# Second angle table from an absolute value on ScalarE, FiLM read from PSUM, and new turns in a two-layer decoder kernel

## The chip, the cores and the metric

The kernel runs on one core of a Trainium2 chip. Its engines are named as the profile names them: PE (TensorE, matrix products), DVE (VectorE), ACT (ScalarE), POOL (GpSimd) and SP (SyncE, which issues DMAs). The metric is the device time of one execution in microseconds; the kernel before took 485.99 us (median of 3 runs, 484.13 to 487.59). Lower is better.

## The reference, cut to what matters

Two sequences of 512 tokens with 128 features go through two post-norm decoder layers. Layer 0: a Hawk recurrent block, cross attention to a short context, and latent attention with a mixture of 7 routed experts and a shared one. Layer 1: a selective scan with 16 states, a state-space cross layer, and a mixture of 8 routed experts and shared ones. After each part stands `x = _layernorm(x + part(x))`. The change lies in the state-space layer:

```
c_t = jnp.einsum('btg,bgd->btd', attn_mean, V)
x = layernorm(x_text, g_norm_in, b_norm_in)
scale_in, shift_in = jnp.split(c_t @ W_film_in + b_film_in, 2, axis=-1)
x = x * (1.0 + mod_gate * scale_in) + mod_gate * shift_in
powers = jnp.exp(dtA[:, :, None] * jnp.arange(L))      # s4d: 64 complex poles per feature
K = 2.0 * jnp.einsum('dn,dnl->dl', dC, powers).real    # 512 taps per feature
y = irfft(rfft(x, n=2 * L) * rfft(K, n=2 * L)) + x * D_skip
scale_out, shift_out = jnp.split(c_t @ W_film_out + b_film_out, 2, axis=-1)
y = y * (1.0 + mod_gate * scale_out) + mod_gate * shift_out
xt = x_text + y
```

The 512 taps K depend on weights alone. [...]

## The kernel before, in words

The two sequences are two **lanes**, a (or 0) and b (or 1); what depends on weights alone is a third, w. A lane's activations stand as 128 features by 512 tokens, in float32, in sixteen tiles of 128 x 512 (`A(b, i)`, in the trace AR; the layer's input is x_in or `Xin`), and each lane owns four banks of PSUM (`own(b, i)`, in the trace PS). RR is a large shared tile that holds the taps' tables and, later, weights.

Each engine's work is a list of named **steps** for each lane (`STEPS`, `STEPS_W`). `TURNS` says for each engine which lane gives its next steps ("a8 w1" is eight steps of lane a, then one of w), and so fixes the engine's order for the whole program; an engine that waits in one lane holds up the others behind it. Every step counts up a semaphore of its engine and lane, and `after(engine, lane, step)` is the wait for it. `TABLES` says ahead of which ACT step a set of activation functions is loaded (42 loads, before as after). Nothing is scheduled at run time.

```
for n, lane in enumerate(lanes_):
    before(n)
    next(programs[lane])
```

Helpers record most instructions on one line each: on ACT L1208 (table loads L1204), on DVE L1553 (two tensors), L1556 (tensor and scalar), L1559 (`stt`, scalar and two tensors), L1562 (reductions), L1565 (reciprocal), L1878 (the selective scan), on POOL L2195 and L2279 (one tensor in pieces of 128 x 512).

**The taps' tables** (lane w, two halves h = 0, 1, each 128 x 1024 and larger). POOL forms angles, `tP` and `tQ`. DVE rounds them to whole turns: `r1`, `q1` (phase 1 into tile p1), `r2`, `q2` (phase 2 into p2), then `rQ0`, `qQ0`, `rQ1`, `qQ1`; an `r` is L1556, a `q` L1559. ACT takes sines (`s1`, `s2`, `sQ`) and exponentials (`eP`, `eQ`). POOL forms `aP`, `aQ`, `U1`, `U2`, `V`, `Q`; DVE `P`. PE sums them to taps (`kp`); taps go through a DMA (`kshuf`, into `Kdl`), PE transposes them (`kt`, L1184) and takes their spectrum (`kf`, L1008).

**The selective scan** of layer 1, per lane and state: ACT an exponential, DMA spreads a row, POOL a product `by` (L2195, after one product `dx`), DVE the scan `sc` (L1878) and a product `hc` (L1553). Lane 1's experts of layer 0 (DVE `hu`, `hw`; PE `fg`, `fu`, `fd`) run beside lane 0's scan, lane 0's state-space layer beside lane 1's scan.

**The state-space layer**, per lane: context attention (`xb.s` ... `xb.p`, whose result is transposed, `xb.t`, L1032); four products with the FiLM weights (`fl0` to `fl3`, L1039), which ACT copies from PSUM with their bias (`s0` to `s3`); DVE `lni.z` and `xin` apply scale and shift to the normed input; PE transposes (`xit`, L1045) and takes the spectrum (`xf`, L1008); DVE multiplies it with the taps' (`xr`, `xi`, `yr`, `yi`, `ye`, `yo`); PE goes back (`inv0`, `inv`, L1061, even and odd tokens in one bank); DVE adds the skip (`sk`, L1559), scales (`fo`), shifts (`fp`) and adds the residual (`xta`, `xt`). The feed-forward part and two layer norms follow (`lnf`, `w1`, `w2`, `lno`, `ln5`; L1067, L1075, L1083, L689), then the second mixture (L1096 its router, L925, L930 and L957 its experts).

## Time and profile before

| What | Value |
|---|---|
| runs | 487.59, 485.99, 484.13 us; median 485.99 |
| profiled execution | 481.76 us; span 480.0 us, 5922 instructions |
| PE busy | 411.1 us (86%) x2035 |
| DVE busy | 331.9 us (69%) x616 |
| ACT busy | 289.2 us (60%) x508, of it 42 table loads 53.9 us |
| POOL busy | 124.9 us (26%) x128 |
| chain that ended last | PE 59%; DVE 21%; ACT 10%; issue 6% |
| mean granted clock of TensorE | 0.932 |

The span runs from the first to the last instruction of the profiled execution; the runs were timed apart from it. A busy share near the length of a stretch says that the engine sets the pace there; the granted clock is a share of TensorE's full speed, so that 0.82 over a stretch means that part of it ran at the lower of its two levels. A row of a timeline may join several like instructions (x2), and its bracket tells how long the engine had been idle and what ended that.

### The profile page before, as it was taken

To read this page: it belongs to the slowest core of one execution; us is meant where nothing else is said; L and a number is where in the kernel's file an instruction comes from. 1 tells how busy PE (TensorE), PEld (TensorE's weight loads), DVE (VectorE), ACT (ScalarE), POOL (GpSimd) and SP (SyncE) were. 2 spreads that over 40 slices of the span, in tenths; PEclk is the share of its full clock that TensorE was granted. 3 is DMA by queue.
4 is the path that set the end of the run, shared out by engine and by line. 5 is a ranking of instruction groups with operands and counts; after the bars stand their busy time and mean duration, and the time that the engine had idled before them with its cause. 6 is when DMAs were issued, how large, how long until landed. Compare 5 with 4: busy or idle time off the path is not lost.

```text
span 480.0 us, 5922 instructions
## 1 busy us (share of the span) xinstructions
PE 411.1 (86%) x2035; PEld 201.5 (42%) x2035; DVE 331.9 (69%) x616; ACT 289.2 (60%) x508; POOL 124.9 (26%) x128
## 2 busy tenths in 40 slices
PE   6978988878799999999977884557889899999995
PEld 3444433443345554434443221233666544544442
DVE  1485567799969963562799999899977543574454
ACT  5945697525255678989567897456347576552125
POOL 1200000000482029006965767745100200000000
PEclk9988999988879999999997998657989999999999
DMA  7950000564281000005008967988600001502401
GB/s 262 362 157 32 1 2 0 164 98 152 70 182 17 2 3 4 2 12 165 0 1 231 233 164 222 217 223 253 252 0 1 1 0 22 156 1 54 124 0 44
DMA packets 26109, 46.62 MB, mean 97 GB/s; under 512 B 7397, under 2 KB 12742, under 8 KB 24918
## 3 DMA queue, kind: packets, MB, share of 16 engines
q1 hardware_dynamic: 25972, 46.15, 33.7%
q8 instruction: 16, 0.26, 0.2%
q10 hardware_dynamic: 108, 0.10, 0.1%
q14 instruction: 13, 0.11, 0.1%
HBM read 41.13 MB, written 5.01 MB: 96 GB/s over the span
## 4 chain that ended last, share of the span: by engine, by line
PE 59%; DVE 21%; ACT 10%; issue 6%; POOL 2%; DMA 1%; DVEq 0%; SPq 0%; ACTq 0%
PE PS L925 7%; DVE AR L1553 7%; PE PS L957 6%; ACT AR L1208 6%; PE PS L930 5%; PE PS L853 4%; PE PS L839 4%; ACT L1204 3%; PE PS L689 3%; PE PS L822 3%; DVE stats L1562 3%; DVE AR L1878 3%; PE PS L1008 2%; PE PS L1061 2%; DVE AR L1559 2%
## 5 line engine op out<-in xcount | busy, mean ns | idle before, releaser
L1208 ACT ACTIVATE AR<-PS 128x512 f32<-128x512 f32 (+1 forms) x219 | 110.6, 537 | 109.1 <-PE PS L925 49.3
L1553 DVE TENSOR_TENSOR AR<-PS,AR 128x512 f32<-128x512 f32 (+1 forms) x104 | 69.1, 675 | 49.6 <-PE PS L930 30.6
L2195 POOL TENSOR_TENSOR AR<-AR 128x512 f32<-128x512 f32 (+2 forms) x48 | 52.3, 1097 | 136.0 <-DVE AR L1553 106.4
L1208 ACT ACTIVATE AR<-AR 128x256 f32<-128x256 f32 (+2 forms) x130 | 54.5, 469 | 44.6 <-DVE AR L1553 28.1
L1204 ACT ACT_TABLE_LOAD x42 | 53.9, 1283 | 0.8
L1562 DVE TENSOR_REDUCE stats<-PS 128x1 f32<-128x512 f32 (+4 forms) x88 | 43.6, 521 | 8.7 <-PE PS L763 3.5
L1878 DVE TENSOR_TENSOR_SCAN AR<-PS,AR 128x512 f32<-128x512 f32 x32 | 38.8, 1211 | 0.7 <-POOL AR L2195 0.6
L822 PE MATMUL PS<-RR 97*128 97x512 bf16 (+3 forms) x128 | 33.3, 337 | 5.5 <-DVE stats L1562 3.6
L689 PE MATMUL PS<-AR,W_sq 128*128 128x256 f32 x88 | 27.3, 424 | 10.6 <-ACT AR L1208 6.3
L1553 DVE TENSOR_TENSOR AR<-AR 128x512 f32<-128x512 f32 (+2 forms) x48 | 30.7, 654 | 3.6 <-ACT AR L1208 2.3
L839 PE MATMUL PS<-RR 100*128 100x512 bf16 (+3 forms) x128 | 29.8, 303 | 2.2 <-ACT AR L1208 2.1
L2279 POOL TENSOR_TENSOR RR<-KL,lags 128x512 f32<-128x512 f32 x24 | 29.4, 1263 | 1.2 <-PE PS L842 1.1
L930 PE MATMUL PS<-x_in,RR 128*128 128x512 f32 x56 | 28.6, 596 | 0.0
L957 PE MATMUL PS<-AR,RR 128*128 128x512 f32 x56 | 28.5, 596 | 0.0
L925 PE MATMUL PS<-x_in,RR 128*128 128x512 f32 x56 | 28.4, 595 | 0.0
L1208 ACT ACTIVATE PS<-AR,RA 128x512 f32<-128x512 f32 x32 | 21.5, 685 | 10.3 <-DMA AR<-scan 5.1
L689 PEld LDWEIGHTS PS<-AR,W_sq 128*128 128x128 f32 x88 | 15.9, 201 | 24.8 <-ACT AR L1208 16.2
L825 PE MATMUL PS<-W_bf 128*128 128x256 bf16 (+1 forms) x80 | 22.4, 280 | 0.0
L853 PE MATMUL PS<-AR,Vaug 128*9 128x512 f32 (+3 forms) x256 | 21.8, 434 | 0.0
L842 PE MATMUL PS<-W_bf 128*128 128x256 bf16 (+1 forms) x80 | 20.2, 253 | 0.0
L1710 DVE TENSOR_REDUCE stats<-PS 128x1 f32<-128x384 f32 x32 | 17.5, 548 | 3.5 <-PE PS L825 3.3
L822 PEld LDWEIGHTS PS<-RR 97*128 97x128 bf16 x128 | 11.5, 105 | 20.0 <-DVE stats L1562 11.0
(239 smaller groups left out, 697.5 us busy)
## 6 DMA issues: line engine op xcount, KB each, us to landing
AR<-scan SPq DMA_DIRECT2D x64, 256.0 KB, 4.0
RR<-in_ffn SPq DMA_DIRECT2D x1, 2688.0 KB, 11.5
RR<-in_ones SPq DMA_DIRECT2D x2, 832.0 KB
RR<-in_ones SPq DMA_DIRECT2D x2, 784.0 KB
RA<-in_moe SPq DMA_DIRECT2D x1, 1539.5 KB, 6.4
AR<-weights SPq DMA_DIRECT2D x6, 256.0 KB, 4.7
W_mla<-in_mla SPq DMA_DIRECT2D x1, 1504.0 KB, 15.3
W_late<-in_late SPq DMA_DIRECT2D x1, 1076.0 KB, 11.8
```

The costliest lines, as they stand in the source:

```text
L689: mm(own(b, i)[:, c], w("sq", "ones"), A(b, 1)[:, c], start=True, stop=True)\
L822: mm(ring[:, c:c + n_], Qst[b][0:MROWS, h, 128 * qt:128 * qt + 128], Kst[b][0:MROWS, h, 0:n_], start=(qt, c) == segs[0][1:], stop=False)
L839: mm(ring[:, c:c + n_], Kst[b][0:KROWS, h, 128 * kb:128 * kb + 128], Qst[b][0:KROWS, h, 128 * kb:T], start=(c == 0), stop=False)
L925: mm(own(b, 0), w(group, "g", 128 * k, 128), x, start=True, stop=True)\
L930: mm(own(b, 1), w(group, "u", 128 * k, 128), x, start=True, stop=True)\
L957: mm(own(b, 3), w(group, "d", 128 * j, 128), A(b, 6 + j % 2), start=(j == 0 and base is None), stop=(k == n))\
L1204: nc.scalar.preload_act_table_set(tables[loaded[0]])
L1208: nc.scalar.activation(out_, in_, func, bias=bias, scale=scale).then_inc(*done("act", *step))
L1553: nc.vector.tensor_tensor(out_, a, b_, op).then_inc(*done("dve", *step))
L1562: nc.vector.tensor_reduce(out_, a, X, op).then_inc(*done("dve", *step))
L1878: nc.vector.tensor_tensor_scan(A(b, 14 + i % 2), own(b, 1 + 2 * (i % 2)), scan_row(b, "dx", i), 0.0, ALU.mult, ALU.add).then_inc(*done("dv ...
L2195: nc.gpsimd.tensor_tensor(out_, a, b_, op).then_inc(*done("pool", *step))
```

## The change

- **Angles.** The DVE steps `r2` and `q2` are gone for both halves. ACT has a new step `ab` per half, 128 x 1024: p2 becomes the absolute value of the sine's argument of phase 1, and `s2` takes the sine of a quarter turn less p2.
- **FiLM.** ACT's copies `s0` and `s1` are gone; `lni.z` and `xin` read the PSUM banks and add the bias themselves. The order is now `fl0`, `fl1`, `fl3`, `fl2`, with `s3` and `s2` still copied by ACT. A new PE step `fx` puts the layer's input into the bank that `fl3` then adds to, so that the shift holds the residual.
- **Skip.** A new DVE step `kD` (128 x 1) adds half of `D_skip` to the first tap after the DMA `kshuf`; `kt` waits for it. The steps `sk`, `fo`, `fp` become `fo0` and `fo` (128 x 256, even and odd tokens, which now come back in two banks), and `xta`, `xt` add the shift with the residual.
- **Orders.** `TURNS` and `TABLES` are new for all engines.

```diff
@@ -63,6 +63,7 @@
               "lnf": (3, 0), "lno": (3, 1), "ln5": (3, 2), "ln6": (1, 0), "lnf.c": (2, 1), "ln5.c": (0, 1)}
+FILM_BANKS, FILM_TURNS = (0, 1, 3, 2), (0, 1, 3, 2)
 
@@ -175,7 +176,7 @@
         *_halves("ln3.v"), "de", "bB", "bC", *[f"yn{i}" for i in range(NS // SUMMED)], "ln4.c",
-        *_halves("ln4.v"), "xb.s", "xb.t", "fl0", "fl1", "fl2", "fl3", "xit",
+        *_halves("ln4.v"), "xb.s", "fx", "xb.t", "fl0", "fl1", "fl3", "fl2", "xit",
         "xf0", "xf1", "inv0", "inv", *_halves("lnf.c"), *_halves("lnf.v"), "w10", "w11", "w12", "w13", "w2", *_halves("lno.v"), *_halves("ln5.c"), *_halves("ln5.v"),
@@ -187,7 +188,7 @@
         "ab", "ex", "sp", "bB", "bC", *[f"aa{i}" for i in _N],
-        *_ln("ln4"), "lni.sq", "lni.l", "lni.r", "xb.e", "lni.g", "xb.a", "s0", "s1", "s2", "s3", "xit", "ko", "xo", *_ln("lnf"), *_halves("lnf.g"),
+        *_ln("ln4"), "lni.sq", "lni.l", "lni.r", "xb.e", "lni.g", "xb.a", "s3", "s2", "xit", "ko", "xo", *_ln("lnf"), *_halves("lnf.g"),
         "u0", "u1", "u2", "u3", *_ln("lno"), *_ln("ln5"), "rt1",
@@ -201,7 +202,7 @@
         "xb.m", "xb.d", "lni.x", "xb.u", "xb.i", "xb.k", "xb.p", "lni.z", "xin", "ks", "kd", "bs", "bd", "xr", "xi", "yr", "yi", "ye", "yo",
-        "sk", "fo", "fp", *_halves("xt"), *_halves("lnf.x"), *_halves("lno.x"), *_halves("s5"), *_halves("X5"),
+        "fo0", "fo", *_halves("xt"), *_halves("lnf.x"), *_halves("lno.x"), *_halves("s5"), *_halves("X5"),
         "mx", "ms", "su", "iv", "pr1", *_PICK1[:5], *_E1[0], *_PICK1[5:9], *_E1[1], *_PICK1[9:],
@@ -209,13 +210,13 @@
     "act": ["fb.a", "fb.e", "fb.l", "dt", "kv0", "kv", "th", "sh", "sy",
-            *[f"{n}{h}" for h in HALVES for n in ("s1", "s2", "sQ", "eP", "eQ", "kp")], "kl"],
+            *[f"{n}{h}" for h in HALVES for n in ("ab", "s1", "s2", "sQ", "eP", "eQ", "kp")], "kl"],
     "dve": ["km", "kb0", "kb1", "tm", *_centre("ws"), "m0a", "m0b", "v0", *_centre("v0"), "k1", "bi", "vr", "m1",
...
             *_centre("w2"), "sz", "hd.s", "hd.m",
-            *[f"{n}{h}" for h in HALVES for n in ("r1.", "q1.", "r2.", "q2.", "rQ0.", "qQ0.", "rQ1.", "qQ1.", "P")],
-            "ed.s", "ed.m"],
+            *[f"{n}{h}" for h in HALVES for n in ("r1.", "q1.", "rQ0.", "qQ0.", "rQ1.", "qQ1.", "P")],
+            "kD", "ed.s", "ed.m"],
     "pool": ["kz", "va0", "va1", "fb.r", "fb.s", "fb.c", "bh", "bf", "bf1", "wz0", "wz1", "la", *[f"dc{i}" for i in range(1, 24)], "wb", "wc", "sz", "hd.c",
@@ the order tables @@
 TURNS = {
     "pe":
-        "a8 w1 a5 w2 a2 w1 a3 w1 a4 w2 a2 b2 a1 b2 a2 b1 a2 b1 a2 b2 a2 b2 a2 b2 a2 b2 a1 b5 a1 b2 a3 b7 a1 b2 "
...
+        "a7 w1 a6 w3 a5 w1 a1 w2 a3 b1 a2 b1 a2 b1 a2 b1 a1 b1 a2 b2 a2 b4 a2 b2 a1 b1 a2 b5 a1 b2 a3 b6 a1 "
...
 TABLES = (
-    "2:log 11:gelu 12:log 14:gelu 17:exp 26:log 40:gelu 47:log 51:gelu 52:exp 64:log 91:gelu 100:log "
...
+    "3:log 11:gelu 13:exp 14:gelu 22:log 40:gelu 47:log 51:gelu 54:exp 65:log 92:sin 93:gelu 101:log "
...
@@ -1027,6 +1028,9 @@
                 yield
+                pe.wait_ge(*after("dve", b, "xb.d"))
+                mm(own(b, 2), w("sq", "id"), Xin[b][:, :], start=True, stop=False).then_inc(*done("pe", b, "fx"))
+                yield
                 pe.wait_ge(*after("dve", b, "xb.p"))
@@ -1035,16 +1039,17 @@
                     pe.wait_ge(*after("act", "w", "kl"))
-                for o in range(4):
-                    mm(own(b, o), VF[:, b, 128 * o:128 * o + 128], A(b, 3), start=True, stop=True)\
+                for o in FILM_TURNS:
+                    mm(own(b, FILM_BANKS[o]), VF[:, b, 128 * o:128 * o + 128], A(b, 3), start=(o != 3), stop=True)\
                         .then_inc(*done("pe", b, f"fl{o}"))
                     yield
+                pe.wait_ge(*after("act", b, "s3"))
                 pe.wait_ge(*after("dve", b, "xin"))
-                pe.wait_ge(*after("act", b, "s3"))
                 for j in range(NT):
...
                 yield
+                pe.wait_ge(*after("act", b, "s2"))
                 pe.wait_ge(*after("act", b, "xit"))
@@ -1058,7 +1063,7 @@
                     for k in range(NFB):
-                        last = mm(own(b, 1)[:, HT * p:HT * p + HT], Yf[b][:, NF * p + 128 * k:NF * p + 128 * k + 128],
+                        last = mm(own(b, (1, 3)[p])[:, HT * p:HT * p + HT], Yf[b][:, NF * p + 128 * k:NF * p + 128 * k + 128],
                                   Gh[:, T * k + p:T * k + T:2], start=(k == 0), stop=(k == NFB - 1))
@@ -1178,7 +1183,7 @@
                     yield
-                pe.wait_ge(kshuf, 16)
+                pe.wait_ge(*after("dve", "w", "kD"))
                 pe.wait_ge(*after("act", "w", "kp1"))
@@ -1456,9 +1461,9 @@
                 act.wait_ge(*after("pool", "w", "bf1"))
-                for o, to in enumerate((4, 5, 6, 8)):
+                for o, to in ((3, 8), (2, 6)):
                     act.wait_ge(*after("pe", b, f"fl{o}"))
-                    f(A(b, to), own(b, o), ACT.Identity, (b, f"s{o}"), bias=bfilm[:, o:o + 1])
+                    f(A(b, to), own(b, FILM_BANKS[o]), ACT.Identity, (b, f"s{o}"), bias=bfilm[:, o:o + 1])
                     yield
@@ -1523,10 +1528,13 @@
                 for h in HALVES:
-                    act.wait_ge(*after("dve", "w", f"q2.{h}"))
+                    act.wait_ge(*after("dve", "w", f"q1.{h}"))
+                    f(tb("p2"), tb("p1"), ACT.Abs, ("w", f"ab{h}"), scale=-TWO_PI, bias=vec("ra1"))
+                    yield
                     f(tb("p1"), tb("p1"), ACT.Sin, ("w", f"s1{h}"), scale=-TWO_PI, bias=vec("ra1"))
                     yield
-                    f(tb("p2"), tb("p2"), ACT.Sin, ("w", f"s2{h}"), scale=-TWO_PI, bias=vec("ra2"))
+                    act.wait_ge(*after("act", "w", f"ab{h}"))
+                    f(tb("p2"), tb("p2"), ACT.Sin, ("w", f"s2{h}"), scale=-1.0, bias=0.25 * TWO_PI)
                     yield
@@ -1918,11 +1926,14 @@
                 yield
-                dve.wait_ge(*after("act", b, "s1"))
-                tt(A(b, 10), A(b, 10), A(b, 4), ALU.mult, (b, "lni.z"))
+                dve.wait_ge(*after("pool", "w", "bf1"))
+                dve.wait_ge(*after("act", b, "lni.g"))
+                dve.wait_ge(*after("pe", b, "fl0"))
+                stt(A(b, 10), own(b, FILM_BANKS[0]), bfilm[:, 0:1], A(b, 10), ALU.add, ALU.mult, (b, "lni.z"))
                 yield
                 mine(b, "lni.z")
-                tt(A(b, 2), A(b, 10), A(b, 5), ALU.add, (b, "xin"))
+                dve.wait_ge(*after("pe", b, "fl1"))
+                stt(A(b, 2), own(b, FILM_BANKS[1]), bfilm[:, 1:2], A(b, 10), ALU.add, ALU.add, (b, "xin"))
                 yield
@@ -1964,21 +1975,14 @@
                 yield
-                dve.wait_ge(*after("pe", b, "inv"))
-                pairs = "p (t two) -> p t two"
-                stt(A(b, 4).rearrange(pairs, two=2), A(b, 2).rearrange(pairs, two=2), vec("Ds"),
-                    own(b, 1).rearrange("p (two t) -> p t two", two=2), ALU.mult, ALU.add, (b, "sk"))
-                yield
-                mine(b, "sk")
-                dve.wait_ge(*after("act", b, "s3"))
-                tt(A(b, 4), A(b, 4), A(b, 6), ALU.mult, (b, "fo"))
-                yield
+                dve.wait_ge(*after("act", b, "s2"))
+                for p in range(2):
+                    dve.wait_ge(*after("pe", b, ("inv0", "inv")[p]))
+                    tt(A(b, 4)[:, p:T:2], own(b, (1, 3)[p])[:, HT * p:HT * p + HT], A(b, 6)[:, p:T:2], ALU.mult, (b, ("fo0", "fo")[p]))
+                    yield
                 mine(b, "fo")
-                tt(A(b, 4), A(b, 4), A(b, 8), ALU.add, (b, "fp"))
-                yield
-                mine(b, "fp")
                 for h, c in COLS:
-                    tt(A(b, 0)[:, c], A(b, 4)[:, c], Xin[b][:, c], ALU.add, (b, f"xt{h}"))
+                    tt(A(b, 0)[:, c], A(b, 4)[:, c], A(b, 8)[:, c], ALU.add, (b, f"xt{h}"))
                     yield
@@ -2169,10 +2173,8 @@
                     yield from turns(tb("p2"), tb("p1"), tb("r"), "ph1", (f"r1.{h}", f"q1.{h}"))
+                    dve.wait_ge(*after("pool", "w", f"tQ{h}"))
                     mine("w", f"q1.{h}")
-                    yield from turns(tb("p2"), tb("p2"), tb("r"), "ph2", (f"r2.{h}", f"q2.{h}"))
-                    dve.wait_ge(*after("pool", "w", f"tQ{h}"))
-                    mine("w", f"q2.{h}")
                     rq = tb("r").rearrange("p d l -> p (d l)").rearrange("p (d l) -> p d l", l=PB_)
@@ -2183,6 +2185,9 @@
                     yield
+                dve.wait_ge(kshuf, 16)
+                stt(Kdl[:, 0:1], vec("Ds"), 0.5, Kdl[:, 0:1], ALU.mult, ALU.add, ("w", "kD"))
+                yield
                 dve.wait_ge(loads["ffn1"], 16)
```

**POOL, the taps' second half and lane 0's scan.** L2279 (L2284 in the change) are pieces of table steps: from KL and lags `tP` and `tQ` (2 and 4 pieces) and `aP`, `aQ` (2 and 4), from RR and KL `U1` and `U2`. AR0 rows are `dx` and `by` of lane 0. Before:

```order
L2279 TENSOR_TENSOR RR<-KL,lags 128x512 x12
L2195 TENSOR_TENSOR AR0<-AR0,x_in0 128x512
L2279 TENSOR_TENSOR RR<-RR,KL 128x512 x2
L2195 TENSOR_TENSOR AR0<-AR0 128x512 x4
L2279 TENSOR_TENSOR RR<-RR,KL 128x512 x2
L2195 TENSOR_TENSOR AR0<-AR0 128x512 x7
L2279 TENSOR_TENSOR RR<-RR 128x512 x2
L2195 TENSOR_TENSOR AR0<-AR0 128x512 x4
```

The change:

```order
L2284 TENSOR_TENSOR RR<-KL,lags 128x512 x6
L2200 TENSOR_TENSOR AR0<-AR0,x_in0 128x512
L2284 TENSOR_TENSOR RR<-KL,lags 128x512 x2
L2200 TENSOR_TENSOR AR0<-AR0 128x512 x5
L2284 TENSOR_TENSOR RR<-KL,lags 128x512 x4
L2200 TENSOR_TENSOR AR0<-AR0 128x512 x3
L2284 TENSOR_TENSOR RR<-RR,KL 128x512 x2
L2200 TENSOR_TENSOR AR0<-AR0 128x512 x2
L2284 TENSOR_TENSOR RR<-RR,KL 128x512 x2
L2200 TENSOR_TENSOR AR0<-AR0 128x512
L2284 TENSOR_TENSOR RR<-RR 128x512 x2
L2200 TENSOR_TENSOR AR0<-AR0 128x512 x4
```

Of the twelve pieces ahead of `dx`, six (`aP1`, `aQ1`) now stand behind it: two right behind `dx`, four between `by4` and `by5`.

**DVE, the taps' second half, lane 0's last layer norm of layer 0 (x_in0) and lane 1's expert choice (stats).** Before:

```order
L1559 SCALAR_TENSOR_TENSOR RR<-RR 128x1024
L1553 TENSOR_TENSOR stats<-PS,W_vec 128x28
L1553 TENSOR_TENSOR x_in0<-PS,AR0 128x256
L1556 TENSOR_SCALAR stats<-stats 128x28
L1553 TENSOR_TENSOR x_in0<-PS,AR0 128x256
L1565 RECIPROCAL stats<-stats 128x28
L1556 TENSOR_SCALAR RR<-RR,W_vec 128x1024
L1553 TENSOR_TENSOR stats<-stats 128x196
L1559 SCALAR_TENSOR_TENSOR RR<-RR 128x1024
L1553 TENSOR_TENSOR stats<-stats 128x196
L1556 TENSOR_SCALAR RR<-RR,W_vec 128x1024
L1553 TENSOR_TENSOR stats<-stats,W_vec 128x196
```

The change:

```order
L1564 TENSOR_SCALAR RR<-RR,W_vec 128x1024
L1567 SCALAR_TENSOR_TENSOR RR<-RR 128x1024
L1564 TENSOR_SCALAR RR<-RR,W_vec 128x1024
L1567 SCALAR_TENSOR_TENSOR AR1<-AR1,W_vec 128x256 x2
L1561 TENSOR_TENSOR x_in0<-PS,AR0 128x256 x2
L1561 TENSOR_TENSOR stats<-PS,W_vec 128x28
L1564 TENSOR_SCALAR stats<-stats 128x28
L1573 RECIPROCAL stats<-stats 128x28
L1567 SCALAR_TENSOR_TENSOR RR<-RR 128x1024
L1564 TENSOR_SCALAR AR0<-PS,W_vec 128x512
L1561 TENSOR_TENSOR stats<-stats 128x196 x2
L1561 TENSOR_TENSOR AR0<-AR0 128x512
```

The roundings `r2` and `q2` (the second and third row on 128x1024 of before) are gone, and the remaining ones up to `rQ0` stand ahead of lane 0's layer norm (x_in0).

**DVE, lane 0's way back from the spectrum beside lane 1's context softmax** (AR0 and AR1 are the two lanes). Before, from `xb.p` of lane 1 on:

```order
L1553 TENSOR_TENSOR AR1<-AR1,stats 128x512
L1559 SCALAR_TENSOR_TENSOR AR0<-AR0,W_vec,PS 128x512
L1553 TENSOR_TENSOR AR0<-AR0 128x512 x2
L1553 TENSOR_TENSOR AR0<-AR0,x_in0 128x256
L1553 TENSOR_TENSOR AR1<-AR1 128x512
L1553 TENSOR_TENSOR AR0<-AR0,x_in0 128x256
L1553 TENSOR_TENSOR AR1<-AR1 128x512
L1562 TENSOR_REDUCE small<-RR 128x14
```

The change, from lane 0's `fo0` on:

```order
L1561 TENSOR_TENSOR AR0<-PS,AR0 128x256
L1570 TENSOR_REDUCE stats<-AR1 128x16
L1573 RECIPROCAL stats<-stats 128x16
L1561 TENSOR_TENSOR stats<-stats,tmaskf 128x16
L1561 TENSOR_TENSOR AR0<-PS,AR0 128x256
L1561 TENSOR_TENSOR AR1<-AR1,stats 128x512
L1561 TENSOR_TENSOR AR0<-AR0 128x256 x2
L1567 SCALAR_TENSOR_TENSOR AR1<-PS,small,AR1 128x512 x2
L1570 TENSOR_REDUCE small<-RR 128x14
```

`fo0` and `fo` of lane 0 now stand ahead of lane 1's `xb.p` (the row AR1<-AR1,stats), and three full tiles of lane 0 have become two halves.

## Rows read from the trace of the kernel before

**Rows 1.** Busy time by stretch: start:end us, length, each engine (instructions), clock, DMA share, GB/s.

```profile
99.00:140.00 41.00, 34.05 (x151) 16.77 (x152) 36.83 (x83) 14.83 (x33) 12.61 (x19) 0.79 0.44 118
...
205.00:240.00 35.00, 32.06 (x129) 13.88 (x127) 19.31 (x39) 27.76 (x39) 20.28 (x17) 1.00 0.19 61
240.00:262.00 22.00, 16.15 (x168) 7.80 (x167) 20.86 (x34) 15.01 (x24) 13.04 (x11) 0.84 0.39 104
262.00:353.00 91.00, 64.22 (x372) 30.85 (x371) 85.13 (x111) 57.61 (x89) 49.66 (x39) 0.82 0.74 212
353.00:386.00 33.00, 30.42 (x130) 20.19 (x129) 20.47 (x37) 19.35 (x40) 3.18 (x1) 0.99 0.00 1
386.00:474.00 88.00, 87.92 (x226) 39.33 (x224) 45.26 (x98) 40.54 (x67) 0.00 (x0) 1.00 0.18 49
```

**Rows 2.** Timeline of DVE, 240 to 262 us: start, duration, instruction [idle before <-releaser].

```profile
241.72 2.07 DVE L1559 SCALAR_TENSOR_TENSOR RR<-RR 128x1024 f32<-128x1024 f32 x1
...
245.22 1.03 DVE L1556 TENSOR_SCALAR RR<-RR,W_vec 128x1024 f32<-128x1024 f32 x1
246.17 1.20 DVE L1553 TENSOR_TENSOR stats<-stats 128x196 f32<-128x196 f32 x1
247.30 1.21 DVE L1559 SCALAR_TENSOR_TENSOR RR<-RR 128x1024 f32<-128x1024 f32 x1
248.44 0.35 DVE L1553 TENSOR_TENSOR stats<-stats 128x196 f32<-128x196 f32 x1
...
255.63 1.22 DVE L1559 SCALAR_TENSOR_TENSOR RR<-RR 128x1024 f32<-128x1024 f32 x1
...
258.95 1.78 DVE L1559 SCALAR_TENSOR_TENSOR RR<-RR 128x1024 f32<-128x1024 f32 x1
260.66 1.21 DVE L1878 TENSOR_TENSOR_SCAN AR<-PS,AR 128x512 f32<-128x512 f32 x1
```

**Rows 3.** Timeline of ACT, 214 to 222 us: two sines.

```profile
216.15 2.19 ACT L1208 ACTIVATE RR<-RR,W_vec 128x1024 f32<-128x1024 f32 x2
```

**Rows 4.** Timeline of POOL, 226 to 280 us.

```profile
231.30 15.86 POOL L2279 TENSOR_TENSOR RR<-KL,lags 128x512 f32<-128x512 f32 x12
...
258.39 1.27 POOL L2195 TENSOR_TENSOR AR<-AR 128x512 f32<-128x512 f32 x1 [2.93 <-DMA AR<-scan]
...
267.18 2.51 POOL L2195 TENSOR_TENSOR AR<-AR 128x512 f32<-128x512 f32 x2
...
274.36 1.28 POOL L2195 TENSOR_TENSOR AR<-AR 128x512 f32<-128x512 f32 x1 [1.17 <-DMA AR<-scan]
276.92 1.28 POOL L2195 TENSOR_TENSOR AR<-AR 128x512 f32<-128x512 f32 x1 [1.29 <-DMA AR<-scan]
```

**Rows 5.** Timeline of DVE, 349 to 386 us.

```profile
355.60 0.75 DVE L1559 SCALAR_TENSOR_TENSOR AR<-AR,W_vec,PS 128x512 f32<-128x512 f32 x1 [0.77 <-PE PS L1061]
356.38 1.42 DVE L1553 TENSOR_TENSOR AR<-AR 128x512 f32<-128x512 f32 x2
...
359.43 0.69 DVE L1553 TENSOR_TENSOR AR<-AR 128x512 f32<-128x512 f32 x1 [1.17 <-ACT AR L1208]
```

**Rows 6.** Timeline of PE, 314 to 337 and 349 to 386 us.

```profile
322.94 1.11 PE L1032 MATMUL PS<-W_sq,AR 128*128 128x128 f32 x4 [3.89 <-DVE AR L1553]
...
356.69 1.98 PE L1039 MATMUL PS<-AR,VF 128*128 128x512 f32 x4 [0.69 <-ACT AR L1208]
...
380.82 1.13 PE L689 MATMUL PS<-AR,W_sq 128*128 128x256 f32 x4 [0.82 <-ACT AR L1208]
382.55 1.13 PE L1067 MATMUL PS<-AR,W_sq 128*128 128x256 f32 x4 [0.60 <-DVE AR L1553]
```

**Rows 7.** Timeline of ACT, 354 to 366 us.

```profile
357.91 1.49 ACT L1208 ACTIVATE AR<-PS,small 128x512 f32<-128x512 f32 x2 [1.28 <-PE PS L1039]
```

**Rows 8.** Timeline of DVE, 76 to 86 us.

```profile
78.85 0.69 DVE L1553 TENSOR_TENSOR AR<-PS,x_in 128x512 f32<-128x512 f32 x1 [0.16 <-PE PS L736]
```

**Rows 9.** Timeline of DVE, 99 to 121 us.

```profile
103.99 0.94 DVE L1565 RECIPROCAL AR<-AR 128x128 f32<-128x128 f32 x1
```

More of the change, by code:

```diff
@@ L226 @@
     "pe":
[7 rows of a table removed]
-    "dve":
[8 rows of a table removed]
-    "act":
[6 rows of a table removed]
[7 rows of a table added]
+    "dve":
[8 rows of a table added]
+    "act":
[6 rows of a table added]
     "pool":
-        "w12 b3 w1 b2 w1 b1 w37 a1 w1 a4 w1 a7 w1 a4 b1 a1 w1 b16 w1",
+        "w34 b2 w2 b1 w2 b3 w11 a1 w1 a5 w1 a3 w1 a2 w1 a1 w1 a4 b1 a1 w1 b16 w1",
 }
 TABLES = (
[4 rows of a table removed]
[4 rows of a table added]
 def steps_of(engine, lane):
```

46 rows, old and new, of tables (TABLES, TURNS) are left out of this document.

## The prediction

> **What bounds the kernel now.** I read the busy time by stretch first, since a share of the whole span mixes stages with different limits. From 240 to 262 us, where the taps' second half, lane 1's expert choice and the start of lane 0's scan meet, DVE is busy 20.86 of 22 us; from 262 to 353, the two scans, 85.13 of 91; PE has slack in both (16.15 and 64.22) [rows 1]. From 353 on it is the other way round: PE is busy 30.42 of 33 and then 87.92 of 88, DVE 20.47 and 45.26. So a DVE microsecond is worth something up to about 353; behind it, only what closes a gap of PE counts: some 2.6 us up to 386, almost nothing after. From 205 to 240 PE (32.06 of 35) leads ACT (27.76) and DVE (19.31). Then I read the timelines of the engines at each edited step [rows 2 to 9].
>
> **Tables, half 1.** On DVE, `r2` took 1.03 and `q2` 1.21, both in the DVE-bound stretch [rows 2]: -2.24 us of DVE work. There is more beside them. `q1` took 2.07 us there, where the same operation on the same shape took 1.22 later; an expert-choice product of 128x196 took 1.20, the next one 0.35; `qQ1` took 1.78 against `qQ0`'s 1.22 [rows 2]. The excesses are 0.85, 0.85 and 0.56, together 2.26. POOL's twelve table pieces ran from 231.30 for 15.86 us [rows 4], so over the first two, and its first scan product (258.39, 1.27) over the third. The new order leaves only six of the twelve ahead of `dx`, so part of the 2.26 can go: between nothing and -2.26. [...]
>
> How much of this reaches the scan? Lane 0's first `sc` began at 260.66 on DVE; its POOL product began at 258.39 after 2.93 us of waiting for a DMA and ended at 259.66 [rows 2, 4]. With that DMA unmoved, DVE gains only 1.00 us there. The DMA follows `dl`, which stood behind `r2` and `q2`, so it can move up by their 2.24; but in the new order `dl` stands behind lane 0's layer norm, which waits for ACT and PE, and two expert-choice products. Bounds -1.0 and -4.5; I take **-1.5**, nearer the DMA's end, since that row has the longest wait.
>
> **Tables, half 0, and ACT.** The same pair on half 0 (at most 2.24) lies where DVE has 15 us to spare before 240: nothing, its cover being PE's work. ACT gains two `ab`; no row shows an absolute value, so I take a sine of the same shape, 2.19 / 2 = 1.10 us [rows 3]. Half 1's lies in a stretch with ACT busy 15.01 of 22: hidden. Half 0's is queued ahead of layer-0 expert activations on an engine with 7 us of slack in 35, and PE needs those: between 0 and +1.1, taken as **+0.3**.
>
> **FiLM and skip, lane 0.** This lies under lane 1's scan on DVE. `lni.z` and `xin` (0.69 each [rows 5]) become operations of `sk`'s kind, with a PSUM operand, 0.75 [rows 5]: +0.12. `kD` is 128x1: bounded by nothing and the smallest full-tile row, 0.69, taken as 0.2. `sk`, `fo`, `fp` (0.75 + 1.42) become two half tiles, which no row has; at half of 0.75 each they take 0.75: -1.4, but near 353, where PE takes over. `kt` now waits for `kD`, itself queued behind a scan step of lane 1, and `fx` precedes `xb.t` on PE; `xb.t` had PE waiting 3.89 us for DVE [rows 6], which covers both. Together **+0.3**, between -1.1 and +1.0.
>
> **FiLM and skip, lane 1 (353 to 386).** PE's gaps to be closed are 0.69 ahead of `fl0`, and 0.82 and 0.60 ahead of the norms that lead to the last router [rows 6]: 2.11 at most. Gone from the chain are the copies `s0`, `s1` (1.49 on ACT [rows 7], for which `lni.z` waited 1.17 [rows 5]) and lane 1's `sk`, `fo`, `fp`. Added to PE is `fx`, 1.98 / 2 = 0.99 from the nearest row, two products of its form [rows 6]. Against the gain stands DVE's order: lane 0's `fo0` and `fo` are now ahead of lane 1's `xb.p`. `xb.p` ended at 354.83 (`sk`'s start, 355.60, less its 0.77 of waiting for PE [rows 5]); behind `fo` it ends at about 355.60 + 0.38 + 0.69 = 356.7, 1.9 later, with lane 1's transposes and FiLM products behind it. That eats what the copies give back. Bounds -1.1 and +1.9; I take **-0.5**: the PE queue has other work to move up, and the gaps before the router are at the end of the shortened chain. Behind 386 the new turns can add only waits, since PE has none; I take nothing, up to +1.
>
> **The first 205 us.** Here only the turns change. Table steps such as the reciprocals of 0.94 us at 103.99 [rows 9] (two of them, with two smaller ones, some 2.8 us as an estimate) move out of 99 to 140, where DVE is busy 36.83 of 41 [rows 1], into its earlier slack. Against them, lane 1's `b.x1`, which waited for PE until 78.85 and takes 0.69 [rows 8], moves ahead of lane 0's last Hawk norm step: about +1.3 on lane 0. Bounds -2.8 and +2; I take **-1.0**.
>
> **Sum.** -1.5 + 0.3 + 0.3 - 0.5 - 1.0 = -2.4 us on the profiled execution's 481.76, so 479.4. The median of the runs shown, 485.99, stands 0.9% above that execution; with the same change the forecast is **483.6**.
>
> **Rivals.**
> *A, the relief lands in full* (faster). With POOL out of DVE's way and `dl` earlier, the scan starts 4.5 us earlier; lane 1's tail gives its 1.1 and the start 1.5; less 0.6 for `ab` and the rest, -6.5: 479.5. For it speaks that DVE has only 6 us of idle time in the 91 of the scans, so that a start moved up stays; against it, the wait for the DMA and that lane 0's norm comes behind ACT.
> *B, the orders give it all back* (no change). The scan gains 1.0, `ab` costs its 1.1, the first stretch nothing, the tail 0: 486. For it: PE's 128 us behind 353 hardly shrink whatever happens ahead of them if lane 1's `xb.p` comes late. It is also the case where the change does not do what it says, an angle table moved from one full engine to another.
> *C, POOL is late for the scan* (slower). `aQ1`, four pieces of 15.86 / 12 = 1.32, 5.3 us, now stands between lane 0's `by4` and `by5`. Before, `by5` ended at 267.18 + 2.51 = 269.69 [rows 4]; a scan step takes 276.92 - 274.36 = 2.56, so `sc5` began near 260.66 + 5 x 2.56 = 273.5, a lead of 3.8. With 5.3 in and two pieces (2.6) out that stood ahead of `by4`, a lead of 1.1 is left, and a scan that starts 1.5 earlier than its products uses it up. From there each further piece is exposed; the price is up to 5.3, and the 1.5 of the scan start is lost too: -2.4 + 1.5 + 5.3 = +4.4, 490.4. Against it: POOL sat idle 1.17 and 1.29 us before the products at 274.36 and 276.92 [rows 4], so it catches up quickly. It decides from a lead of zero at `by5`.
>
> **Chances.** Forecast 0.42 (own range 481 to 486), A 0.22, B 0.20, C 0.16. About 1%, 4.9 us, is what a measurement of this kernel can tell from no change. Under 481.1 lie most of A and some of the forecast: 0.27. Over 490.9 lie nearly half of C and a tail of B, in which the unknowns of the early orders add up: 0.13. The rest, 0.60, is within 1%. The range takes in A's middle and half of C: 478.5 to 490.0, which leaves out some 0.06 below and 0.13 above.
>
> **What would show it.** In the profile after: `q1` of half 1 and the 128x196 product at 1.2 and 0.35 us (relief) or stretched still; the first lane-0 scan step at about 259 us relative to the start of the table stretch, and what it waited for, DVE's own queue or POOL; DVE idle before `sc5` with POOL as releaser (C); lane 1's `xb.p` some 2 us behind lane 0's `inv`; PE's gaps before the last router at under 1 us together; PE still without gaps behind it. The prediction is wrong if the time lies outside the range, if the scan starts more than 3 us earlier or any later, or if the difference turns out to lie ahead of 205 us, where I worked with bounds only.

## The result, and the profile after

The changed kernel took 490.77 us (median of 4 runs, 486.58 to 492.46) against 485.06 us of the kernel before (4 runs, 481.59 to 487.59): ratio 1.0113, 95% interval 1.0057 to 1.0170. It is slower; 483.6 was forecast, within 478.5 to 490.0. Run again later beside the kernel before, in more runs, the ratio was 1.0043, interval 1.0006 to 1.0080: slower still, by less. Ratios are taken over undisturbed runs, so that they can differ from the quotient of the medians.

Its profiled execution spans 490.2 us, 10.2 more than that of before. Both orders have done the same steps, to within seven of some 1,700, at these places (seams below), so that the span can be cut there: 95, 180, 218, 302, 370 us before, and 95, 187.5, 227, 312.5, 380 after. The stretches are 0, 7.5, 1.5, 1.5, -0.5 and 0.2 us longer. Busy time by stretch of the changed kernel (columns as in [rows 1]; lane 0's maxima end at 141 us before and at 150 after):

```profile
95.00:150.00 55.00, 46.36 (x183) 21.55 (x183) 43.10 (x95) 17.02 (x35) 19.99 (x32) 0.67 0.49 114
150.00:187.50 37.50, 36.74 (x330) 19.68 (x331) 27.29 (x68) 24.74 (x47) 2.45 (x2) 1.00 0.01 3
...
227.00:312.50 85.50, 65.23 (x303) 26.44 (x299) 67.80 (x97) 62.43 (x91) 58.66 (x51) 0.90 0.53 147
312.50:380.00 67.50, 53.05 (x371) 33.13 (x372) 56.29 (x81) 34.11 (x62) 19.91 (x16) 0.82 0.56 165
...
398.00:484.00 86.00, 85.08 (x220) 38.24 (x218) 45.74 (x93) 40.68 (x66) 1.30 (x1) 1.00 0.18 51
```

From 95 to 150 us PE's granted clock averages 0.67 (0.81 before on 95 to 141), and DVE is busy 43.10 of 55 us. From 398 on PE is busy 85.08 of 86: still the bound there, with 0.9 us of gaps.

DVE from `q1` of half 1 to the fourth scan step of lane 0, which answers to [rows 2]:

```profile
249.61 1.23 DVE L1567 SCALAR_TENSOR_TENSOR RR<-RR 128x1024 f32<-128x1024 f32 x1
...
257.48 0.62 DVE L1561 TENSOR_TENSOR stats<-stats 128x196 f32<-128x196 f32 x2
...
259.06 1.31 DVE L1561 TENSOR_TENSOR stats<-stats 128x196 f32<-128x196 f32 x1
...
267.13 1.22 DVE L1886 TENSOR_TENSOR_SCAN AR<-PS,AR 128x512 f32<-128x512 f32 x1 [1.46 <-POOL AR L2200]
...
270.32 2.06 DVE L1561 TENSOR_TENSOR AR<-PS,AR 128x512 f32<-128x512 f32 x3
...
274.59 0.69 DVE L1561 TENSOR_TENSOR AR<-PS,AR 128x512 f32<-128x512 f32 x1 [1.08 <-ACT AR L1213]
```

`q1` takes 1.23 (2.07 before) and two of the 128x196 products 0.62 together (one took 1.20): the relief came. Another such product now takes 1.31. The first scan step, at 267.13, waits 1.46 us for POOL; behind the second step, DVE works on `hu1`, `hw1` (two of the three at 270.32), which stood ahead of the scan before, and at 274.59 it waits for ACT.

POOL, the answer to [rows 4]:

```profile
258.83 1.32 POOL L2200 TENSOR_TENSOR AR<-AR,x_in 128x512 f32<-128x512 f32 x1 [10.06 <-DVE AR L1561]
260.11 2.19 POOL L2284 TENSOR_TENSOR RR<-KL,lags 128x512 f32<-128x512 f32 x2
265.77 1.26 POOL L2200 TENSOR_TENSOR AR<-AR 128x512 f32<-128x512 f32 x1 [3.47 <-DMA AR<-scan]
...
274.26 4.06 POOL L2284 TENSOR_TENSOR RR<-KL,lags 128x512 f32<-128x512 f32 x4
```

`dx`, then `aP1` (2.19), 3.47 us of waiting for the DMA, `by0`, and `aQ1` behind `by4` in 4.06 us, not the 5.3 that I had from the pieces before. The product that stretched on DVE (259.06) ran beside `dx`.

PE and DVE in the state-space layer, lane 0 from 333 and lane 1 from 364 us, the answers to [rows 5, 6]; L1189 is `kt`, L1032 `fx`, L1036 `xb.t`, L1066 the way back:

```profile
333.20 1.13 PE L1189 MATMUL PS<-W_sq,stats 128*128 128x128 f32 x4 [4.47 <-DVE stats L1567]
334.13 1.91 PE L1032 MATMUL PS<-x_in,W_sq 128*128 128x512 f32 x2
...
365.59 1.02 PE L1032 MATMUL PS<-x_in,W_sq 128*128 128x512 f32 x2
366.87 0.66 PE L1036 MATMUL PS<-W_sq,AR 128*128 128x128 f32 x4 [0.26 <-DVE AR L1561]
...
390.73 0.70 PE L1072 MATMUL PS<-AR,W_sq 128*128 128x256 f32 x2 [0.48 <-DVE AR L1561]
...
393.65 0.70 PE L690 MATMUL PS<-AR,W_sq 128*128 128x256 f32 x2 [0.49 <-ACT AR L1213]
```

```profile
364.02 0.43 DVE L1561 TENSOR_TENSOR AR<-PS,AR 128x256 f32<-128x256 f32 x1 [1.49 <-PE PS L1066]
...
365.79 0.43 DVE L1561 TENSOR_TENSOR AR<-PS,AR 128x256 f32<-128x256 f32 x1 [0.26 <-PE PS L1066]
366.13 0.68 DVE L1561 TENSOR_TENSOR AR<-AR,stats 128x512 f32<-128x512 f32 x1
...
369.47 1.58 DVE L1567 SCALAR_TENSOR_TENSOR AR<-PS,small,AR 128x512 f32<-128x512 f32 x2 [1.99 <-PE PS L1043]
```

`kt` waited 4.47 us for `kD`. `fx` took 1.91 us at the lower clock (granted clock 0.50 from 333 to 336 us) and 1.02 at the higher (1.00 from 365 to 367). `fo0`, at 364.02, held DVE 1.49 us until PE's first half came, with lane 1's softmax behind it; lane 1's `xb.p` ran at 366.13, behind `fo`. PE's gaps ahead of the router are 0.48 and 0.49.

ACT's absolute value on half 0, the price that no row had:

```profile
207.74 1.15 ACT L1213 ACTIVATE RR<-RR,W_vec 128x1024 f32<-128x1024 f32 x1
```

It took 1.15 us; 1.10 was taken for it.

### The profile page after: what moved, and what is told of

It reads as the page before. It is cut to its first block, busy times and chain, and to the rows that moved or that the text cites. A ratio compares the mean times of both kernels' runs of the same rounds, so it can differ in the third digit from the quotient of the medians.

```text
span 490.2 us, 5927 instructions
## 1 busy us (share of the span) xinstructions
PE 419.9 (86%) x2039; PEld 203.7 (42%) x2039; DVE 326.0 (67%) x611; ACT 288.1 (59%) x506; POOL 120.9 (25%) x128
## 4 chain that ended last, share of the span: by engine, by line
PE 60%; DVE 18%; ACT 11%; issue 4%; DMA 4%; POOL 1%; SPq 0%; DVEq 0%; ACTq 0%
ACT AR L1213 7%; PE PS L926 7%; PE PS L931 6%; PE PS L958 6%; DVE AR L1561 5%; DVE stats L1570 4%; PE PS L854 3%; PE PS L690 3%; PE PS L840 3%; DMA AR<-scan 3%; PE PS L727 3%; DVE AR L1567 3%; PE PS L1009 2%; ACT L1209 2%; PE PS L1066 2%
## 5 line engine op out<-in xcount | busy, mean ns | idle before, releaser
L1213 ACT ACTIVATE AR<-PS 128x512 f32<-128x512 f32 (+2 forms) x219 | 110.0, 536 | 109.1 <-PE PS L926 46.3
L1561 DVE TENSOR_TENSOR AR<-PS,AR 128x512 f32<-128x512 f32 (+1 forms) x108 | 70.9, 667 | 61.1 <-PE PS L931 25.4
L1570 DVE TENSOR_REDUCE stats<-PS 128x1 f32<-128x128 f32 (+4 forms) x88 | 43.8, 524 | 13.0 <-PE PS L764 5.1
L823 PE MATMUL PS<-RR 97*128 97x512 bf16 (+3 forms) x128 | 35.4, 356 | 4.3 <-DVE stats L1570 3.9
L2284 POOL TENSOR_TENSOR RR<-KL,lags 128x512 f32<-128x512 f32 x24 | 24.9, 1073 | 25.2 <-PE PS L843 25.1
L1561 DVE TENSOR_TENSOR AR<-AR 128x512 f32<-128x512 f32 (+3 forms) x44 | 26.9, 626 | 2.5 <-ACT AR L1213 0.9
L826 PE MATMUL PS<-W_bf 128*128 128x256 bf16 (+1 forms) x80 | 23.4, 293 | 0.0
L843 PE MATMUL PS<-W_bf 128*128 128x256 bf16 (+1 forms) x80 | 20.2, 252 | 0.0
```

The lines of the kernel that those rows point to most:

```text
L823: mm(ring[:, c:c + n_], Qst[b][0:MROWS, h, 128 * qt:128 * qt + 128], Kst[b][0:MROWS, h, 0:n_], start=(qt, c) == segs[0][1:], stop=False)
L1213: nc.scalar.activation(out_, in_, func, bias=bias, scale=scale).then_inc(*done("act", *step))
L1561: nc.vector.tensor_tensor(out_, a, b_, op).then_inc(*done("dve", *step))
L1570: nc.vector.tensor_reduce(out_, a, X, op).then_inc(*done("dve", *step))
```

## The experiments

Theory 1: the new order of the start (95 to 150 us) loses the time. Theory 2: the edits do. Theory 3: the new order behind that does. Theory 4, added later: TensorE's granted clock does. "Old order" below means the changed code with each new step where the old one stood.

**All of the order, and none of it.**

```diff
 TURNS, TABLES (changed code)
-the new order
+the old order; w.ab ahead of w.s1, kD behind a.xb.i, fx ahead of xb.t, fo0 at sk, fo at fo
```

> The changed code (absolute value on ScalarE, FiLM read from PSUM, skip in the first tap) in the order of the kernel before; the new steps stand where the old ones stood. Theory 1, the new turns of the first 150 us lose the time (lane 0's last maximum step ends 8.7 us later there): without them the kernel is no slower than before, 481 to 486 us, ratio 0.99 to 1.00. Theory 2, the edits themselves lose it (an absolute value on a full ScalarE, waits for the first tap): about 490 us, ratio 1.01. Theory 3, the new order from 205 us on loses it: 481 to 486 here too, and the run with only the old start tells it from theory 1.

Measured: 483.39 us, ratio 0.9999 (0.9963 to 1.0035). Theory 2 falls: the edits alone neither gain nor lose beyond 0.4%.

```diff
 TURNS, TABLES (code of before)
-the old order
+the new order; r2, q2 behind q1, sk, fo, fp at the place of fo
```

> The converse: the code of the kernel before in the new order, with the removed steps put back behind their neighbours. Theory 1 and theory 3 (turns): 490 to 496 us, ratio 1.01 to 1.02, with the last maximum step of lane 0 some 8 us later than before. Theory 2 (edits): 485 us, ratio 1.00.

Measured: 500.94 us, ratio 1.0327 (1.0249 to 1.0404), more than any theory said. The new order is bound to the new steps: with three full tiles ahead of lane 1's `xb.p` its trace falls behind by 4.6 us between 302 and 356 alone. It shows that order loses here, not how much of it the change pays.

**The start.**

```diff
 changed code, each engine
-new order to 141 us of the old one
+old order to 141 us, then the new one
```

> The changed kernel with the old order up to 141 us of the profile before (the end of lane 0's maxima) and the new order behind it. Theory 1: the 8.7 us come back but for what waits later, 480 to 484 us, ratio 0.99 to 1.00. Theory 3 (later turns): 488 to 491 us, ratio 1.01. Theory 2 (edits): 488 to 491 us too.

Measured: 495.71 us, ratio 1.0262 (1.0215 to 1.0309). This run tells nothing on the theories: at 141 us the two orders have done different steps (25 of them), and at the seam PE was busy 4 of 10 us while lane 1's maxima fell behind by 9.5 us. Later cuts were made where the orders agree.

```diff
 code of before, each engine
-old order to the end of lane 0's maxima
+new order to there, then the old one
```

> The kernel before with the new order up to the end of lane 0's maxima and the old one behind it. Theory 1: as slow as the changed kernel or a little more, 490 to 495 us, ratio 1.01 to 1.02. Theories 2 and 3: 485 us, ratio 1.00.

Measured: 487.36 us, ratio 1.0092 (1.0066 to 1.0117). For theory 1, it seemed; but of the 5.3 us by which its trace is longer only 2.5 are there at 150 us, and the others come between 302 and 356, where nothing was changed.

```diff
 changed code, each engine
-old order to 182 us
+new order to 182 us (187.5 of its own), then the old one
```

> The changed code with the new order up to the middle of the attention (182 us of the old order, 187.5 of the new; the orders have done the same steps there to within one) and the old order behind it. If the start alone carries what the middle (+0.5%) does not: 487 to 490 us, ratio 1.008 to 1.015, as the kernel before with the new order to 150 us (1.009). If the loss of the whole change needs the new start and the new middle together: 484 to 486, ratio 1.000 to 1.005.

Measured: 483.83 us, ratio 1.0006 (0.9972 to 1.0041). With the changed code the start alone loses nothing that can be measured: theory 1 falls. One reservation: these runs stood at granted clocks of 0.942 on average, those of the kernel before beside them at 0.933, so that a small loss could hide behind the clock; no run separates the two. Why the kernel before pays for the same start stays open. Two places of the start were tried by themselves, in the old order:

```diff
 PE
-mx0.A xa.t0 mx0.B mx0.C mx0.D xa.t1 mx0.E mx1.A xa.o
+mx0.A mx0.B mx0.C xa.t0 mx0.D xa.t1 mx0.E xa.o mx1.A
 DVE
-xa.i0 xa.p0 xa.u1 xa.i1 mx0.A xa.p1 mx0.B mx0.C a4 mx0.D mx0.E mx1.A s2a s2
+mx0.A mx0.B xa.i0 mx0.C xa.p0 xa.u1 xa.i1 xa.p1 a4 mx0.D mx0.E s2a s2 mx1.A
```

> The changed code in the old order but for one place: lane 1's context attention stands between lane 0's maxima as in the new order (two more maxima ahead of its products on DVE, its transposes two groups later and its last product one group earlier on PE). If this place carries theory 1's loss: 485.5 to 488 us, ratio 1.005 to 1.01, with lane 0's step mx1.E 3 to 4 us later than in the old order. If the loss lies in lane 1's projections ahead of mx3.B instead: 483.4 us, ratio 1.00.

Measured: 483.72 us, ratio 0.9978 (0.9946 to 1.0011), with mx1.E only 0.2 us later than in the old order: not here.

```diff
 PE
-mx3.A mx3.B b.lat mx3.C mx3.D mx3.E mx4.A mx4.B b.kf b.q0 b.q1 mx4.C
+mx3.A b.lat b.kf b.q0 b.q1 mx3.B b.v mx3.C mx3.D mx3.E mx4.A mx4.B mx4.C
 DVE
-mx3.A mx3.B
+mx3.A b.k1 b.k2 b.q1 b.q2 mx3.B
```

> The changed code in the old order but for one place: lane 1's projections of the latent attention (lat, kf, q0, q1 and, on DVE, the four products on them) stand in one block ahead of lane 0's maxima mx3.B, as in the new order. If this block carries the start's loss: 486 to 488 us, ratio 1.005 to 1.01, with DVE idle 3 us or more ahead of the block and lane 0's mx3.E some 6 us later. If what is lost at mx3.E is given back by mx5.E, since PE then has the maxima in one piece: 483 to 485 us, ratio 1.00.

Measured: 482.79 us, ratio 0.9996 (0.9952 to 1.0039). DVE did wait ahead of the block:

```profile
119.25 2.48 DVE L1561 TENSOR_TENSOR AR<-PS,W_mla 128x512 f32<-128x512 f32 x4 [3.06 <-PE PS L794]
```

mx3.E came 5.6 us later than the trace stood just before, 2.8 of it was back by mx5.E, and all by 150 us: a wait that the next stretch gives back, as the second expectation had it.

**One stretch at a time, the rest in the old order.**

```diff
 changed code, each engine
-old order from 182 to 302 us
+new order there
```

> The changed code in the old order, with the new order only between 182 us and the end of lane 0's scan (302 us); both seams are places where the two orders have done the same steps to within one. Theory 1 (the loss is in the start, 95 to 150 us): no slower than the changed code in the old order, 482 to 486 us, ratio 0.995 to 1.005. Theory 3 (the new order around the tables and the scan loses): 487 to 492 us, ratio 1.01 to 1.02. If the relief of DVE from POOL and the earlier tables are worth anything, it shows here: 480 to 482.

Measured: 487.2 us, ratio 1.0053 (1.0025 to 1.0080). Theory 3 holds for this stretch. Busy time of all engines from 182 to 250 us, first in the old order, then in this run:

```profile
182.00:250.00 68.00, 62.15 (x485) 28.70 (x484) 34.85 (x66) 53.18 (x94) 39.84 (x34) 1.00 0.11 33
```

```profile
182.00:250.00 68.00, 61.27 (x490) 27.52 (x482) 30.07 (x60) 52.81 (x95) 30.70 (x28) 1.00 0.11 33
```

PE did 0.9 us less; DVE did 30.07 us of work instead of 34.85. Of these 4.8 us, 0.8 are there because this trace was 0.8 us later at 182 already; the other 4.0 were put off to where DVE is the bound, and lane 0's last scan step ends 4.0 us later (both set at 182 us).

```diff
-old order from 302 to 356 us
+new order there
```

> The same with the new order only between 302 and 356 us (lane 1's scan and lane 0's state-space layer). Theory 1: 482 to 486 us, ratio 0.995 to 1.005. Theory 3, applied here: 487 us or more. The profile of the changed code in the old order showed PE waiting 3.4 us for the first tap's sum here; the new order puts that step later still behind a scan step, so a loss of 1 us is possible under both.

Measured: 479.97 us (4 runs), ratio 0.9893 (0.9829 to 0.9957): a gain. `kt` waits for `kD` in both orders; PE in the old order, then in this run:

```profile
322.04 1.13 PE L1190 MATMUL PS<-W_sq,stats 128*128 128x128 f32 x4 [3.36 <-DVE stats L1568]
```

```profile
322.98 1.13 PE L1190 MATMUL PS<-W_sq,stats 128*128 128x128 f32 x4 [5.41 <-DVE stats L1568]
```

`kt` is even later behind lane 1's scan steps, so the gain is not there. What is earlier is lane 0's way back. DVE in the old order, then in this run (L1571 is lane 1's `xb.m`):

```profile
353.68 0.69 DVE L1571 TENSOR_REDUCE stats<-PS 128x16 f32<-128x512 f32 x1 [0.32 <-PE PS L1029]
354.40 0.69 DVE L1562 TENSOR_TENSOR AR<-PS,stats 128x512 f32<-128x512 f32 x1
355.01 0.68 DVE L1562 TENSOR_TENSOR AR<-x_in,AR 128x512 f32<-128x512 f32 x1
355.61 0.68 DVE L1562 TENSOR_TENSOR AR<-AR 128x512 f32<-128x512 f32 x1
```

```profile
349.90 1.28 DVE L1562 TENSOR_TENSOR AR<-AR 128x512 f32<-128x512 f32 x2
351.62 0.69 DVE L1571 TENSOR_REDUCE stats<-PS 128x16 f32<-128x512 f32 x1 [0.44 <-PE PS L1029]
```

In the old order lane 0's `yo` (355.61) stands behind three steps of lane 1's softmax, 2.0 us, and their wait for PE; in the new one (the second of 349.90) ahead of them. Set at 302 us, `yo` ends 3.5 us earlier, but PE's way back only 2.1, and so does all that PE does until the end. Over the kept traces of the changed code, `yo` ends 47.9 to 50.2 us behind lane 0's last scan step in the new order and 50.5 to 56.0 in the old; PE's way back ends 52.7 to 55.2 and 52.7 to 58.1 us behind it. The earlier `yo` is in every trace; how much of it reaches PE is not shown by a single pair.

```diff
-old order from 356 us
+new order there
```

> The same with the new order only from 356 us on (lane 1's state-space layer and the last mixture). Theory 1: 482 to 487 us, ratio 0.995 to 1.007, since PE has no gaps to lose in the old order and only what the new one adds counts. Theory 3 for this stretch: 488 us or more.

Measured: 483.63 us, ratio 0.9972 (0.9937 to 1.0008): nothing lost.

```diff
-old order from 302 us
+new order there to the end
```

> The changed code with the old order up to the end of lane 0's scan (302 us) and the new order from there to the end: the two pieces that were no slower by themselves (ratios 0.989 and 0.997). If they add: 477 to 480 us, ratio 0.985 to 0.99, faster than both kernels. If the tail, which PE bounds, takes back what comes earlier: 483 us, ratio 0.995 to 1.00.

Measured: 482.52 us, ratio 0.9981 (0.9937 to 1.0024). The gain of the stretch to 356 is not seen here, as the second expectation had it; or the four runs of that kernel lie low, since the intervals overlap.

**POOL's turns alone.**

```diff
 POOL: tP1 tQ1
-aP1 aQ1 dx U11 by0 by1 by2 by3 U21 by4 by5 by6 by7 by8 by9 by10 V1
+dx aP1 by0 by1 by2 by3 by4 aQ1 by5 by6 by7 U11 by8 by9 U21 by10 V1
```

> The changed code in the old order but for POOL's, which is the new one for the taps' second half and lane 0's scan: two pieces behind dx, four between by4 and by5. Rival A's mechanism (POOL out of DVE's way): DVE's q1 of half 1 at 1.2 instead of 2.1 us and the 128x196 product at 0.35, the scan's start 1 to 2 us earlier, 481 to 483 us, ratio 0.995 to 1.00. Rival C's mechanism (POOL late for the scan): DVE idle ahead of lane 0's sc5 with POOL as releaser, 485 to 488 us, ratio 1.003 to 1.01.

Measured: 481.65 us, ratio 0.9930 (0.9886 to 0.9973). Rival A's mechanism is there, rival C's is not: the scan starts 1.3 us earlier than in the old order (both set at 182 us). DVE and POOL of this run:

```profile
236.91 1.53 DVE L1565 TENSOR_SCALAR RR<-RR,W_vec 128x1024 f32<-128x1024 f32 x1
...
242.78 1.22 DVE L1568 SCALAR_TENSOR_TENSOR RR<-RR 128x1024 f32<-128x1024 f32 x1
...
245.45 0.64 DVE L1562 TENSOR_TENSOR stats<-stats 128x196 f32<-128x196 f32 x2
246.00 0.75 DVE L1565 TENSOR_SCALAR RR<-RR,W_vec 128x1024 f32<-128x1024 f32 x1
...
256.73 1.77 DVE L1568 SCALAR_TENSOR_TENSOR RR<-RR 128x1024 f32<-128x1024 f32 x1
258.43 1.21 DVE L1887 TENSOR_TENSOR_SCAN AR<-PS,AR 128x512 f32<-128x512 f32 x1
```

```profile
256.16 1.26 POOL L2201 TENSOR_TENSOR AR<-AR 128x512 f32<-128x512 f32 x1 [3.58 <-DMA AR<-scan]
...
264.64 4.06 POOL L2285 TENSOR_TENSOR RR<-KL,lags 128x512 f32<-128x512 f32 x4
```

`q1` took 1.22 us and two 128x196 products 0.64. Of the three stretched rows only `qQ1` is still at 1.77, beside `by0` (256.16 to 257.42), as before [rows 2, 4]. The rule of the Trainium skill (SBUF — State Buffer, section Who interferes with whom), that a DVE instruction with two SBUF inputs contends with a GpSimd instruction that reads SBUF, agrees with all three. Two inputs are not the whole of it: `r1` reads one large tile of SBUF (and a column of constants) and took 1.53 us beside the pieces of `tP1` and `tQ1` (236.91), where the same operation took 0.75 without POOL (246.00). `aQ1`'s four pieces took 4.06 us, and no scan step waited for `by5`.

**The whole, and what does not add.** By its pieces the change should have been no slower, so it was run again.

```diff
 nothing: the changed kernel
```

> The changed kernel itself once more, in more runs beside the kernel before on one chip. By its pieces (start 1.00, middle 1.005, 302 to 356 0.99, tail 0.997, each against the kernel before) it should be no slower: 481 to 486 us, ratio 0.995 to 1.003. If the first result (1.011) holds, 488 to 491 us, the pieces do not add, and the loss is in how one stage meets the next. Theory 4: the loss is in the granted clock of TensorE, which was 0.916 and 0.920 in the slower of the changed kernel's first runs and 0.932 in the faster ones; then the runs of it fall along their clock, about 486 at 0.935.

Measured: median 489.14 us of 12 runs, ratio 1.0043 (1.0006 to 1.0080). The ten runs in the ratio, at mean clocks of 0.932 to 0.941, took 484.1 to 490.2 us, in no order of the clock: within that narrow range theory 4 does not account for the loss. Two of the first four runs, 492.05 and 492.46 us, stood lower, at 0.916 and 0.920; part of the difference between 1.0113 and 1.0043 may lie there, which no run tests.

```diff
-old order to 302 us
+new order to there, then the old one
```

> The changed code with the new order to the end of lane 0's scan and the old one behind it. If the start and the middle add: 1.00 x 1.005, 485 to 488 us. If the new start makes the new middle worse (lane 1 comes later out of the start, and the middle works on lane 0 first): 489 to 493 us, ratio 1.01 to 1.02.

Measured: 489.2 us, ratio 1.0069 (1.0037 to 1.0101).

```diff
-new order to 182 us
+old order to there, then the new one
```

> The changed code with the old order to 182 us and the new one from there. If the pieces add (1.005, 0.99, 0.997): 480 to 483 us, ratio 0.99 to 0.997. If the middle and what follows do not add: 487 to 491 us, ratio 1.005 to 1.015, and the whole loss of the change lies behind 182 us.

Measured: 485.26 us, ratio 1.0008 (0.9975 to 1.0041). New order to 302 (1.0069) times new order from 302 (0.9981) is 1.0050, beside 1.0043 for the whole: within their intervals the pieces add, and the loss stands ahead of 302, in the middle above all.

```diff
 old order
+POOL's new turns; new order from 302 to 356 us
```

> The changed code in the old order with the two pieces of the new order that gained by themselves: POOL's turns in the tables and lane 0's scan (0.993), and all engines' between 302 and 356 us (0.989). If both gains stand beside each other: 474 to 478 us, ratio 0.98 to 0.987. If the first is lost where PE takes over, as most of a scan that starts 3 us earlier was: 478 to 481 us, ratio 0.988 to 0.993.

Measured: 480.8 us, ratio 0.9911 (0.9873 to 0.9948): faster than both kernels, though less than the product of its parts (0.982).

**Where in the middle.**

```diff
-old order from 182 to 218 us
+new order there
```

> The changed code in the old order with the new order only between 182 and 218 us, where both lanes end the attention of layer 0. In the run with the new order from 182 to 302 us lane 0 came out of the attention 3 to 4 us earlier and lane 1 some 4 us later, and DVE did 30.1 us of work up to 250 us instead of 34.9; behind that it is the bound. If this place carries the middle's loss: 487 to 490 us, ratio 1.006 to 1.012. If the work put off comes from the turns behind 218: 483 to 485 us, ratio 1.00.

Measured: 486.32 us, ratio 1.0024 (0.9986 to 1.0062): inconclusive by itself.

```diff
-old order from 219 to 302 us
+new order there
```

> The complement: the new order only between 219 and 302 us (tables, lane 0's scan, POOL's turns among them). If the loss lies ahead of 218: as fast as with POOL's new turns alone, 479 to 483 us, ratio 0.99 to 0.997. If it lies here: 486 to 490 us, ratio 1.005 to 1.012.

Measured: 485.87 us, ratio 1.0037 (1.0003 to 1.0071). POOL's turns are in this stretch and gain 0.7% alone, so that by the middle values the turns of the other engines lose about 1% in it. DVE and ACT of this run:

```profile
258.08 1.22 DVE L1886 TENSOR_TENSOR_SCAN AR<-PS,AR 128x512 f32<-128x512 f32 x1 [1.63 <-POOL AR L2200]
...
265.56 1.89 DVE L1561 TENSOR_TENSOR AR<-PS,AR 128x512 f32<-128x512 f32 x3 [1.11 <-ACT AR L1213]
```

```profile
262.92 0.69 ACT L1213 ACTIVATE PS<-AR,RA 128x512 f32<-128x512 f32 x1 [2.47 <-DMA AR<-scan]
263.63 1.28 ACT L1209 ACT_TABLE_LOAD   x1
264.93 0.60 ACT L1213 ACTIVATE AR<-PS 128x512 f32<-128x512 f32 x1
```

The scan starts 1.6 us earlier than in the old order (both set at 182 us), the gain that was forecast. By `sc5` it is 1.7 us behind: the first step waited 1.63 us for POOL, `hu1` and `hw1` of lane 1 come behind `sc1`, and `hu2`, at 265.56, waits for ACT. Two things hold ACT's step there (264.93): lane 1's expert choice now ends 2.8 us later, behind lane 0's layer norm and the table steps; and on ACT two more exponentials of lane 0's scan stand ahead of it, of which the second (262.92) waited 2.47 us for its DMA and was followed by a table load.

The traces also tell where the loss arises. Lane 0's last scan step in four runs: the old order, POOL's turns alone, the new order from 219 us, the new order from 182 us:

```profile
301.80 1.21 DVE L1887 TENSOR_TENSOR_SCAN AR<-PS,AR 128x512 f32<-128x512 f32 x1
...
298.56 1.21 DVE L1887 TENSOR_TENSOR_SCAN AR<-PS,AR 128x512 f32<-128x512 f32 x1
...
301.42 1.21 DVE L1886 TENSOR_TENSOR_SCAN AR<-PS,AR 128x512 f32<-128x512 f32 x1
...
306.63 1.21 DVE L1886 TENSOR_TENSOR_SCAN AR<-PS,AR 128x512 f32<-128x512 f32 x1
```

Against the first, the others stood 1.9 and 2.0 us earlier and 0.8 us later at the end of lane 1's maxima, where all four are still in the old order. With that taken off, the scan ends 1.3 us earlier with POOL's turns alone, 1.6 us later with the new order from 219 us, and 4.0 later with it from 182; five more traces in the old order lie within 0.4 us of the first. So some 2.4 us are lost ahead of 219, and behind it the other engines' turns lose 2.9, if POOL's give back there the 1.3 that they give alone.

## Why the prediction was wrong

- **The bounds** were read rightly: DVE to about 353 us, PE behind it.
- **The step that failed is "how much of this reaches the scan"**, with its -1.5 us, and rival A's reason for keeping it, that DVE has only 6 us of idle time behind the start. The start did move up. In the changed kernel the first scan step is 3.2 us earlier against lane 0's `X3` (9.7 us late at `X3`, 6.5 at `sc0`), and 2.5 earlier against the seam at 218 us, which is 9 late; but at `sc5` it is 9.9 late and at the last scan step 10.1, so that the scan ends 1.1 us later against that seam. I measured when the scan begins, not how much DVE work is left behind that point. The new order moved work of lane 1 from ahead of the scan into it, and left DVE idle ahead of it: from the end of lane 1's maxima to the end of `sc0` DVE was busy 42.3 of 85.6 us with the new order from 182 us, 46.4 of 84.8 in the old. Where an engine is the bound, only idle time taken out, or work taken out, shortens the stretch. The middle cost 0.5% in place of my -0.3%.
- **The relief of DVE**, taken as 0 to 2.26 us inside that -1.5, came: with POOL's turns alone the scan starts and ends 1.3 us earlier than in the old order, and the kernel gains 0.7% (1.3 to 5.5 us by the interval). That the excess would go with the moved pieces was right. That `dx` would stretch another row in its place (259.06) was missed, and so was that one-input operations are stretched too: `r2`'s 1.03 [rows 2] stands against 0.75 without POOL.
- **The first 205 us**, -1.0 within -2.8 and +2: the profiled execution lost 7.5 us by 187.5 us; the runs say 1.0006 for this stretch alone. I had the terms but no way to see that lane 1's projections would stand in one block ahead of lane 0's maxima, and the run on this block shows that it gives back what it costs. The turns from 182 to 218, which lose some 2.4 us at the scan's end, got no term of their own.
- **"`xb.t` had PE waiting 3.89 us for DVE, which covers both"** was wrong: `kt` itself waits, 4.47 us in the changed kernel and 3.36 in the old order. It cost little: all edits together give 0.9999, where my terms for them (-1.5 + 0.3 + 0.3 - 0.5, of which the first counts POOL's turns too) would give 0.9971, inside the interval.
- **Lane 1's tail** was right in its parts: `xb.p` ends at 366.81 behind `fo`, `fx` takes 1.02, and PE's gaps before the router come to 0.97 us, with 0.26 ahead of `xb.t`. PE had 0.9 us of gaps behind 398.
- **Rival C** did not come: `aQ1` took 4.06 us, not 5.3, and POOL was late for `sc0`, not for `sc5`. Its lead was over-read: before, `sc5` began at 272.25, not 273.5, so that the lead was 2.6 us, not 3.8. The slower side came from DVE's, ACT's and the lanes' order, which no rival named.
- **Left open:** the 0.7% between the two measurements of the change, whose intervals overlap; why the new start costs 0.9% in the kernel before and nothing that can be measured in the changed one; which step between 182 and 218 us loses the time.

## What to carry to other kernels

In a stretch that one engine bounds, count its idle time and its work on either side of a cut; the time at which the stretch begins says little when the order has moved work across it. To price a new order, put it in one stretch at a time, with cuts where both orders have done the same steps. Moving the second engine's work away from the bound engine's operations gained 0.7% here (ratio 0.9930), where the edits by themselves gained nothing that can be measured (0.9999); the two intervals just overlap. And look at every engine that feeds the stretch: a step of one lane queued behind a step of the other that waits for a DMA holds up the bound engine as well.

## What the runs showed of the hardware

The same program gets TensorE's lower clock at different places in different executions. The changed kernel's two profiled executions, first then again, from 130 to 150 us:

```profile
130.00:150.00 20.00, 17.44 (x87) 7.46 (x85) 19.90 (x47) 5.51 (x10) 7.18 (x9) 0.62 0.69 159
```

```profile
130.00:150.00 20.00, 17.37 (x105) 8.13 (x106) 19.25 (x49) 6.39 (x12) 5.38 (x7) 0.83 0.67 154
```

PE was about as busy in both, 17.44 and 17.37 us, at granted clocks of 0.62 and 0.83. Lane 0's maxima ended 8.7 us later than before in the first and 4.9 in the second: a single trace's difference of some us in this stretch is no property of an order.
